# The end of the first attention: VectorE multiplies the band factor of the last slot, and feed-forward's first unit is prepared ahead of it

## The reference

```python
x = x + 0.5 * L0_ffn(layernorm(x))       # s = x Win + bin; h = relu(s*W1 + b1), 16 per s; g = sum h*W2 + b2; g Wout + bout
x = x + L0_attn(layernorm(x))            # 16 heads of 8; scores/sqrt(8) + 0.1 where |i-j| <= 2; softmax; @ v; @ Wo
x = x + 0.5 * L0_ffn(layernorm(x))
x = x + 0.5 * L1_ffn(layernorm(x))       # FP4 quantised linears, silu(gate)*up
x = x + L1_attn(layernorm(x))            # causal, latent keys and values
x = x + 0.5 * L1_ffn(layernorm(x))
```

## Time and profile before

| | us |
|---|---|
| median of 3 runs | 506.68 (506.49 to 509.33) |
| the profiled execution, its own time | 506.44 |
| span of that execution, first to last instruction | 504.6 |
| PE busy | 418.7 (83%) |
| DVE busy | 350.3 (69%) |
| POOL busy | 305.0 (60%) |
| ACT busy | 285.1 (56%) |

### The profile page before, as it was taken

One profiled execution on the slowest core, in us unless ns is written; L12 is line 12 of the kernel. 1 busy time (PEld: TensorE's weight loads), 2 busy tenths in 40 slices (PEclk: granted clock), 3 DMA queues, 4 the chain that ended last, 5 costly groups with the idle time before them and its releaser, 6 DMA issues.

```text
span 504.6 us, 11467 instructions
## 1 busy us (share of the span) xinstructions
PE 418.7 (83%) x3693; PEld 268.9 (53%) x3693; DVE 350.3 (69%) x882; ACT 285.1 (56%) x521; POOL 305.0 (60%) x585
## 2 busy tenths in 40 slices
PE   3996889999999967685788478799999998767975
PEld 1453425666666643343456355567766765334654
DVE  5769686888778644874899637857676776148992
ACT  5774515666666755657885135235455546668741
POOL 5314336777777770546898325346666677679961
PEclk9999957999999999987999679759999999579997
DMA  6001793332333000000000004973323330000001
GB/s 196 1 2 47 173 271 82 96 97 76 85 82 96 5 2 0 2 0 1 1 1 2 1 0 136 254 182 91 86 78 89 95 97 3 2 2 0 22 21 43
DMA packets 31122, 31.77 MB, mean 63 GB/s; under 512 B 4954, under 2 KB 26330, under 8 KB 31075
## 3 DMA queue, kind: packets, MB, share of 16 engines
q1 hardware_dynamic: 31074, 31.18, 23.2%
HBM read 21.30 MB, written 9.44 MB: 61 GB/s over the span
## 4 chain that ended last, share of the span: by engine, by line
PE 53%; DVE 14%; POOL 13%; issue 10%; ACT 6%; DMA 2%; SPq 1%; DVEq 0%; POOLq 0%; ACTq 0%
PE psum L639 6%; PE psum L293 4%; POOL hq L1175 4%; PE psum L593 3%; PE psum L623 3%; POOL hb_v L1170 3%; PE psum L594 2%; PE psum L596 2%; DVE nm L729 2%; PE psum L613 2%; PE psum L643 2%; DVE nm L732 2%; DVE xn L228 2%; PE psum L614 2%; PE psum L416 2%
## 5 line engine op out<-in xcount | busy, mean ns | idle before, releaser
L688 ACT ACTIVATE h_sb<-psum 128x1024 f32<-128x1024 f32 (+1 forms) x128 | 110.7, 914 | 52.8 <-PE psum L614 26.8
L729 DVE TENSOR_REDUCE nm<-psum 128x2 f32<-128x512 f32 x128 | 82.3, 685 | 14.0 <-PE psum L594 12.8
L732 DVE TENSOR_REDUCE nm<-psum 128x3 f32<-128x384 f32 x128 | 65.7, 552 | 11.3 <-PE psum L600 9.3
L698 POOL TENSOR_TENSOR h_sb<-h_sb,bandw 128x512 f32<-128x512 f32 x48 | 61.0, 1270 | 0.0
L234 POOL TENSOR_TENSOR rstd<-veps,mhalf 128x4 f32<-128x4 f32 (+1 forms) x32 | 28.3, 884 | 45.0 <-DVE veps L220 43.6
L639 PE MATMUL psum<-h_sb,v_b 128*32 128x256 f32 x512 | 44.0, 416 | 4.2 <-POOL h_sb L698 4.1
L766 DVE RECIPROCAL rsum<-psum 128x16 f32<-128x16 f32 x32 | 8.2, 258 | 49.7 <-PE psum L655 49.7
L702 POOL TENSOR_SCALAR_AFFINE_SELECT h_sb<-h_sb 128x512 f32<-128x512 f32 x64 | 40.8, 638 | 0.0
L593 PE MATMUL psum<-kst,qst 72*128 72x256 bf16 x128 | 36.0, 298 | 3.4 <-DVE nm L729 2.5
L596 PE MATMUL psum<-kst,qst 72*128 72x128 bf16 x128 | 30.2, 236 | 7.8 <-DVE nm L732 6.5
L594 PE MATMUL psum<-kst,qst 72*128 72x256 bf16 x128 | 36.1, 298 | 0.0
(11 more groups left out here) (234 smaller groups left out, 1158.3 us busy)
## 6 DMA issues: line engine op xcount, KB each, us to landing
qst<-q_dram SPq DMA_DIRECT2D x96, 96.0 KB
kst<-k_dram SPq DMA_DIRECT2D x96, 96.0 KB
q_dram<-q_parts SPq DMA_DIRECT2D x16, 192.0 KB, 3.2
k_dram<-k_parts SPq DMA_DIRECT2D x16, 192.0 KB, 3.5
k_dram<-k_parts SPq DMA_DIRECT2D x16, 128.0 KB, 3.6
x<-in_L_attn_x SPq DMA_DIRECT2D x4, 256.0 KB, 4.5
out_x<-x SPq DMA_DIRECT2D x4, 256.0 KB, 2.3
pk<-in_packed SPq DMA_DIRECT2D x1, 689.5 KB, 5.8
```

The source lines that it names most:

```text
L688: nc.scalar.activation(pexp[p][:, :, 0:w], psum[:, 4 + 2 * (p % 2):6 + 2 * (p % 2), 0:w], ACT.Exp, scale=scale).then_inc(sem("a_exp"), 1)
L698: ins = nc.gpsimd.tensor_tensor(wide, wide, bandw[:].unsqueeze(1).unsqueeze(1).to_broadcast([P, 2, 2, P]), ALU.mult)
L729: nc.vector.tensor_reduce(nm[slot % 2][:, HEAD[h]], bank[e].rearrange("p (t k) -> p t k", t=2), AX.X, ALU.max, negate=True).then_inc(sem(" ...
L732: nc.vector.tensor_reduce(nm3[slot % 2][:, HEAD[h]], bank[e][:, 0:3 * P].rearrange("p (t k) -> p t k", t=3), AX.X, ALU.max, negate=True).t ...
```

## The change

Four things, all at this seam.

1. In slot 3 of the last quad DVE multiplies the band factor (`dve_mask`, the same two products on the same tiles) and raises a semaphore of its own, a_mskd, for which `pe_values` waits there. POOL has no masks in that slot.
2. The stats and norm of ffn_b's unit 0, and the stats of its unit 1, are written around slot 2 (`lead`, "stats" and "norm"): DVE's first stats stand ahead of slot 1's `dve_norm`, POOL's power stands between its second and third mask, DVE's norm at the end of slot 2.
3. In `back`, PE does unit 0's transposes before the last value group and its s before `pe_ouT`; ACT does the matching copies around `act_ou` and the hidden pairs after `act_oT`. DVE does its whole step 1 of ffn_b, and only then the last `dve_y`.
4. Unit 0 of ffn_b uses the second of each pair of buffers (`flip`), so that its hidden pairs don't go to h_sb[0], where pexp still lives; the two PSUM banks of g swap as well. The waits at the entry of PE's steps are moved accordingly.

```diff
-                ph[which](eng, k + ph["first"], k % 2, lambda lag: 0 <= k - lag < ph["n"])
+                ph[which](eng, k + ph["first"], (k + ph.get("flip", 0)) % 2, lambda lag: 0 <= k - lag < ph["n"])
...
+            gb = (2, 3) if inst == 0 else (3, 2)
...
+            def lead(eng, which, part):
+
+                nu, tu, par = nu0, tu0, 1
+                at = (which, part)
+                if at == ("dve", "stats"):
+                    ln_stats(eng, nu, par, 0, 4, x_ready(0))
+                if at == ("pool", "stats"):
+                    ln_pool(eng, nu, par, 4)
+                if at == ("dve", "norm"):
+                    ln_norm(eng, nu, par, 0, 4, [("xT_ps", tu)])
+                    ln_stats(eng, nu + 1, 1 - par, 4, 4, x_ready(1))
+                if at == ("pool", "norm"):
+                    ln_pool(eng, nu + 1, 1 - par, 4)
+                if at == ("pe", "xT"):
+                    eng.wait_ge(sem("a_max"), HH * 16)
+                    xT_pe(eng, nu, tu, par)
+                if at == ("act", "xT"):
+                    xT_act(eng, tu, par, "f_sps", f0 - 1)
+                if at == ("pe", "s"):
+                    pe_s(eng, f0, par)
+                if at == ("act", "s"):
+                    act_s(eng, f0, par)
+                if at == ("act", "h"):
+                    act_hidden(eng, f0, par)
+                if at == ("dve", "next"):
+                    dve_body(eng, f0 + 1, 0, lambda lag: 0 <= 1 - lag < 4)
...
+            def dve_mask(dve, p):
+
+                dve.wait_ge(sem("a_exp"), PR * 15 + p + 1)
+                wide = pexp[p].rearrange("p e (t c) -> p e t c", c=P)[:, :, 0::3]
+                edge = pexp[p][:, :, P:3 * P].rearrange("p e (t c) -> p e t c", c=BAND)[:, :, 0::P - 1]
+                nc.vector.tensor_tensor(edge, edge, bande[:].unsqueeze(1).to_broadcast([P, 2, 2, BAND]), ALU.mult)
+                nc.vector.tensor_tensor(wide, wide, bandw[:].unsqueeze(1).unsqueeze(1).to_broadcast([P, 2, 2, P]),
+                                        ALU.mult).then_inc(sem("a_mskd"), 1)
...
+                    if final_band:
+                        dve_mask(eng, 0)
+                        dve_mask(eng, 1)
                     if has_prev:
                         dve_norm(eng, *prev)
+                    if final_band:
+                        dve_mask(eng, 2)
...
                 if which == "pe":
-                    pe_values(eng, *last, 1)
-                    pe_ouT(eng, *last)
+                    if ffn:
+                        ffn["lead"](eng, which, "xT")
+                    pe_values(eng, *last_slot, 1)
+                    if ffn:
+                        ffn["lead"](eng, which, "s")
+                    pe_ouT(eng, *last_slot)
...
-                          {("pe", 0): [("a_max", HH * 16)],
-                           ("pe", 1): [("a_y", 8), ("a_exp", PR * 16)]}, {4: 0, 5: 1, 6: 2})
+                          {("pe", 1): [("a_ou", 16)],
+                           ("pe", 2): [("a_y", 8), ("a_exp", PR * 16)]}, {4: 0, 5: 1, 6: 2})
```

More of the change, by code:

```diff
@@ L14 @@
 import numpy as np
+from functools import partial
 import concourse.bass as bass
@@ L292, in pe_g @@
                     for half in range(2):
[L293 removed]
+                        last = nc.tensor.matmul(bank[gb[par]][M * half:M * half + M, 0:256], dw2[:, p], h_sb[par][:, p, 256 * half:256 * half + 256],
                                                 start=(p == 0), stop=(p == NPAIR - 1))
@@ L632, in pe_values @@
                     wait(pe, "a_ou", 4 * qd + slot)
-                pe.wait_ge(sem("a_msk"), m0 + MASKED[inst] * 4 * (qd - q0) + (MASKED[inst] * slot + min(2 * g + 2, MASKED[inst])))
+                if l0 and isinstance(qd, int) and (qd, slot) == last_slot:
+                    pe.wait_ge(sem("a_mskd"), min(2 * g + 2, MASKED[inst]))
+                else:
+                    pe.wait_ge(sem("a_msk"), m0 + MASKED[inst] * 4 * (qd - q0) + (MASKED[inst] * slot + min(2 * g + 2, MASKED[inst])))
                 if 2 * g + 2 > MASKED[inst]:
@@ L790, in neighbour, with unit @@
                 return (qd + (slot + by) // 4, (slot + by) % 4)
-            def unit(eng, which, qd, slot, has_prev, has_prev2, has_1, has_2, has_3):
+            def unit(eng, which, qd, slot, has_prev, has_prev2, has_1, has_2, has_3, extra=lambda point: None):
+                extra("begin")
                 prev, prev2, n1, n2, n3 = (neighbour(qd, slot, k) for k in (-1, -2, 1, 2, 3))
@@ L801, in unit @@
                         sp_rows(eng, *n1)
-                if which == "pool":
+                final_band = l0 and not has_1
+                if which == "pool" and not final_band:
                     pool_mask(eng, qd, slot, 0)
                     pool_mask(eng, qd, slot, 1)
+                    extra("mask1")
                     if has_2 and slot % 2 == 0:
@@ L865, in unit @@
                             dve_causal(eng, *n2)
-            last = (q0 + 3, 3)
+                extra("end")
             def saved(sp, c):
@@ L910, in front, with quad @@
                     pool_split(eng, q0, slot)
-            def quad(eng, which, n, beside):
+            def quad(eng, which, n, beside, final=lambda slot, point: None):
                 if which == "sp" and n < 2:
@@ L926, in quad, with back @@
                         beside(slot)
-                        unit(eng, which, q0 + 3, slot, True, True, slot < 3, slot < 2, slot < 1)
-            def back(eng, which):
+                        unit(eng, which, q0 + 3, slot, True, True, slot < 3, slot < 2, slot < 1, partial(final, slot))
+            def back(eng, which, ffn=None):
                 if which == "pe":
-                    pe_values(eng, *last, 1)
-                    pe_ouT(eng, *last)
-                if which == "act":
-                    act_ou(eng, *last)
+                    if ffn:
[4 more added lines that the diff above has]
+                    pe_ouT(eng, *last_slot)
+                if which == "act":
+                    if ffn:
+                        ffn["lead"](eng, which, "xT")
+                    act_ou(eng, *last_slot)
+                    if ffn:
+                        ffn["lead"](eng, which, "s")
                 if which == "dve":
-                    dve_norm(eng, *last)
+                    dve_norm(eng, *last_slot)
                 if l0:
@@ L943, in back @@
                         act_oT(eng, q0 + 3, 1)
+                        if ffn:
+                            ffn["lead"](eng, which, "h")
                     if which == "dve":
+                        if ffn:
+                            ffn["lead"](eng, which, "next")
                         dve_y(eng, q0 + 3, 1)
@@ L1442, in entrance, with attention_then_ffn, final @@
                     at["front"](eng, which, 1)
-            def next_ffn(slot):
-                if slot == 3 and which in ("dve", "pool"):
-                    step(eng, which, ffn_b, 0)
+            def attention_then_ffn(at, then):
+                def final(slot, point):
+                    if (which, slot, point) in (("dve", 2, "begin"), ("pool", 2, "mask1")):
+                        then["lead"](eng, which, "stats")
+                    if (which, slot, point) in (("dve", 2, "end"), ("pool", 2, "end")):
+                        then["lead"](eng, which, "norm")
+                for n in (0, 1, 3):
+                    at["quad"](eng, which, n, lambda slot: None, final=final)
+                at["back"](eng, which, then)
             def next_fp4(slot):
@@ L1464, in program @@
             entrance(proj_a, attn_a)
[L1465 to L1468, removed]
+            attention_then_ffn(attn_a, ffn_b)
+            if which != "dve":
+                run(ffn_b, 1, 2)
+            run(ffn_b, 2, 3)
             for k in range(3):
```

28 lines of the change are left out of this document (16 added, 12 removed).

## The result

| | before | changed |
|---|---|---|
| median of 20 runs each | 509.02 (505.25 to 514.82) | 504.12 (498.37 to 509.12) |
| profiled execution, its time | 506.44 | 504.17 |
| its span | 504.6 | 502.4 |
| its mean granted clock | 0.910 | 0.896 |

The ratio is 0.9905 with a 95% interval of 0.9878 to 0.9932: 4.8 us faster, between 3.5 and 6.2. It compares the means, 508.1 and 503.3 us, of the runs that lie within 1.5% of each kernel's fastest (17 and 16 of the 20). The three runs shown before the prediction had a median of 506.68; with 20 runs it is 509.02.

What follows compares the result with a forecast made beforehand. The seam was taken as bound by order and latency, not by any engine's throughput. Values 3.3 plus ladder 2.9 minus 0.3 gives 5.9 us: 506.68 - 5.9 = 500.8, range 498.8 to 503.6.

Steps and rivals of the forecast that it cites:

- Masks to VectorE: Slot 3: a mask costs 0.75 us on VectorE; first value group 2.5 us earlier, second 3.3.
- Rival (a): Slot 3: VectorE's masks cost 1.39 us each plus 0.6 waiting behind the power; gain 3.7, time 503.0; chance 0.12.
- Stats and norm around slot 2: Slot 2: unit 0's stats in idle time, norm 2.0 us from 179.85, third mask later but with 0.8 us cover left.
- The ladder: Second value group's end to VectorE's first hidden pair: 3.3 us against 6.2, a gain of 2.9.
- The last addition to x: Behind the weight steps, ahead of unit 2's norm: costs 0.3 us of its 0.42.
- The clock of the tail: Seam: TensorE's gap shrinks from 3.1 to about 0.6 us, so full clock is kept.
- Rival (b): Tail of the seam: low clock stays or comes back; gain 3.4, time 503.3; chance 0.12.
- (c): Feed-forward, transposes at 215.93: that low-clock stretch goes too, some 1.3 us less, time 499.5; chance 0.17.
- later stages the same, 5.9 us earlier: Sign for everything after the seam: unchanged stages, each starting 5.9 us earlier.
- Behind it, masks and norms have moved and nothing was added: After unit 2's norm: no further cost charged beyond the 0.3 us for the last addition to x.
- Rival (e): FP4 stage: later stages stay longer at the lower clock, 1.3 us per stretch, 511 with eight stretches; chance 0.05.
- The forecast of more than 1%: Whole kernel: faster by over 1% (5.07 us, a time of 501.6), given chance 0.65.

Runs made afterwards that it cites:

- the control of the kernel before: The kernel before, run again with nothing changed: median 510.74 us over 12 runs, ratio 1.0033.
- the order alone: Changed kernel with slot 3's masks kept on GpSimd and unit 1's power behind them: ratio 0.988, 9.58 us from slot 3's first exponential to VectorE's first hidden pair.
- the shortest seam with extra matmuls: Changed kernel with GpSimd's masks first, unit 0's transposes and slot 3's turn earlier, extra matmuls at the second attention's entrance: 501.46 us, ratio 0.9834.

## Why the prediction was wrong

The mechanism at the seam was right. Forecast 5.9 us by the norm of unit 2; measured 23.19 from the first exponential before and 16.89 after, 6.3. Against the control of the kernel before, whose ladder ran at the lower level, it is 8.6 (25.45); the prediction knew only the other case. By terms, against the first trace:
- *Masks to VectorE*: wide product 0.68 against 0.685 taken; first value group within 0.1 us of the schedule. Rival (a) did not happen: the first wide product (184.73) ran beside the power (from 184.49) and was not held for 0.6 us.
- *Stats and norm around slot 2*: the norm took 2.22 in place of 2.0 and the third mask hid as said.
- *The ladder*: 2.90 us from s to the hidden pair (188.83 to 191.73) against 3.3, so 0.4 shorter than summed; 0.18 of that is s to turn, 0.96 and not 1.14, since the two overlap at their ends (s lasts until 189.95, the turn starts at 189.79).
- *The last addition to x*: the lead shrinks from 6.75 at the hidden pair to 6.30 at the norm's start and 6.41 at its end: 0.34 against 0.3.
- *The clock of the tail*: full, as taken, in the seam of all seven traces that have both the lead and early masks. Rival (b) did not happen, and (c) neither: the lower level sits at unit 2 now (201.30, 1.09 for the transposes), where it sat at unit 3 (215.93, which the prediction calls unit 2).

Two steps failed. The larger is the level: "against the median the forecast is 506.68 - 5.9 = 500.8". I took three runs as the kernel's level, and 0.2 us between two of them as its spread. Over all groups the medians of the kernel before were 509.0 to 512.4, its single runs 505.1 to 517.6. From 509.02 the same 5.9 gives 503.1; the level is 2.3 of the 3.3 us by which 504.12 misses 500.8.

The other is "later stages the same, 5.9 us earlier", with "Behind it, masks and norms have moved and nothing was added": a term put at nothing. The seam alone gave 6.3 or 8.6 us, the whole kernel 4.8 to 4.9, so 1.4 to 3.8 us of it didn't arrive. In the traces of the two unchanged kernels the part from the second attention on is 4.2 and 4.4 us longer with the change (179.1 and 179.2 against 174.9 and 174.8), at a mean clock of 0.66 and 0.65 against 0.81 in both from 300 to 345. That 5.9 lies inside the measured gain of 3.5 to 6.2 is in part luck: a seam that gave more than forecast and a later part that took some of it back. The range, built from terms of the seam alone, had no room for either step.

Rival (e), at 0.05, had this mechanism: later stages at the lower clock for longer. It did not come out slower, but the mechanism moves the total by 4 to 5 us from one execution to the next, more than most parts of this change. As a measure of the seam, the comparison of the two profiled spans (2.2 us) would have misled by a factor of three. The forecast of more than 1% was too sure as well: the ratio is 0.95% below one.

The reason that I gave for the masks' cost was only half of it. They were late since they stood behind a power that waited for stats; that VectorE's product is cheaper (0.68 against 1.27) brought nothing that the order alone did not (9.58 against 9.91).

What stays open is what decides how long the low stretch at the second entrance lasts, and whether the change shifts how often the longer one comes. No experiment controls it.

## What to carry to other kernels

Before an instruction goes to another engine, look at what stands ahead of it in its own list: moving one unrelated power of 1 us behind the urgent masks gave 2.8 us here, without any work for another engine. A wait of 3 us on TensorE cost 1 to 3 us more here in the work that follows, so gaps should be closed first where a ladder of dependent steps comes next. Compare local marks in the traces, and take a level and a spread from many runs before a forecast in absolute time is given.

## What the runs showed of the hardware

- A VectorE norm (one input, all in SBUF) next to GpSimd's wide product waited for its end: four of them took 2.22 us (1.10 alone), three starting only when that product ended at 182.15.
- A VectorE product with two SBUF inputs waited too, in the second attention, beside GpSimd's causal mask on h_sb: 0.34 us where it takes 0.17 alone (316.13), ending 0.02 us behind the mask (349.31 and 349.29). The changed kernel's timeline:

```profile
316.13 0.17 DVE L786 TENSOR_TENSOR nm<-nm 128x8 f32<-128x8 f32 x1
...
348.97 0.34 DVE L786 TENSOR_TENSOR nm<-nm 128x8 f32<-128x8 f32 x1
...
348.65 0.64 POOL L740 TENSOR_SCALAR_AFFINE_SELECT h_sb<-h_sb 128x512 f32<-128x512 f32 x1
```

- GpSimd's power held neither form: beside it (184.49 to 185.50) the wide product of two SBUF inputs took 0.68 us, as without it, and the power took its usual 1.01; a VectorE step with one input (L1046, 128x384) took 0.36 wholly within another power. The Trainium skill ("SBUF — State Buffer", "🔬 SBUF: two separate sides") has a VectorE operation with two SBUF inputs and a GpSimd operation that reads SBUF exclude each other for the whole instruction. The row at 348.97 agrees; the power, which reads two SBUF tensors of four columns, does not, and it is the only partner that the masks of this change met.
- TensorE stayed at the lower level for 20 us (0.50 from 320 to 340) while it was busy for 19.56 of them.
- One execution of the shortest seam with extra matmuls ran at a mean clock of 0.723 and took 546.6 us; all others of that kernel lay between 497 and 503.
